# Fused local/global attention and top-1 expert layer on one core: the values' normalisation moved from TensorE's f32 transposes to VectorE's 32x32 block transposes

## The chip, the core and the metric

The kernel runs on one core of a Trainium2 chip. The metric is the device time of one execution in microseconds, the median of several. Unchanged, three runs gave a median of 1819.14 us (1817.94 to 1822.35).

## What is computed

The reference, cut to what matters here (x is 16 x 512 x 256, so 8192 tokens of 256 features):

```python
def mha(x, W_in, b_in, W_out, b_out, mask):      # 16 heads of 16
    q, k, v = heads(split(x @ W_in.T + b_in))
    scores = einsum('bhqd,bhkd->bhqk', q, k) / 4 + mask
    a = softmax(scores)
    o = einsum('bhqk,bhkd->bhqd', a, v)
    return o @ W_out.T + b_out
# local: windows of 128 tokens; global: windows of 256
fused = w[0] * local + w[1] * global             # w = softmax(fusion_w)
y = layernorm(fused) * gamma + beta
x = x + layernorm(y)
# then a top-1 mixture of 32 experts, 320 slots each, and x + layernorm(...)
```

All of it is f32 at the edges. The change touches only o: the quotient of the weighted values and the softmax denominators, in both attentions.

## The kernel before, in words

There are 32 windows of 256 tokens. The attention part is a software pipeline of 36 steps. In step s five windows are in work: `a` = s is projected to queries and keys, `b` = s-1 gets its row maxima and its value projection, `c` = s-2 gets scores, exponentials and the products with the values, `d` = s-3 gets the output projection and its two normalisations, `f` = s-4 gets router and slots. Steps 4 to 31 have all five. After the steps, 32 experts follow, which the change does not touch.

Each step is cut into 24 units k (`UNITS`). In unit k every engine walks through the same list of jobs, each job at the unit that the table `AT` (L271) or `GROUP_AT` (L276) gives it. Each engine's program is in order, so this hand-written table sets what waits behind what. A unit's frame is: TensorE makes a bank of scores of `c` (`scores`, L1091), then the jobs of that unit, then a bank of raw scores of `b` (`row_scores`, L1158); VectorE does its jobs and then the maximum of that bank (`maximum`, L883); ScalarE does the exponential of the first bank (`exps`, L674). The raw-score banks are two, so TensorE's `row_scores(k)` waits for VectorE's `maximum(k-2)`.

The values. For each window eight groups of four heads (four local, four global) are multiplied by TensorE into one PSUM bank, `PV`, [4 heads x 32 rows, 256 tokens]; of the 32 rows of a head 16 are the values and one is the softmax denominator (`values`, L1121). In the kernel before, ScalarE copies each group to `OT` (`values_out`, L676, line L681). TensorE transposes four groups at a time, 128 tokens, into bank `TR` (`norm_T`, L1202; four f32 transposes through L1184), VectorE takes the reciprocals of the denominators and multiplies (`normalise`, L899, lines L903 and L907), TensorE transposes back, four more (`out_T`, L1207), and ScalarE copies the result to `OnT` (`onT_out`, L726, line L730). The output projection `op` (L1275, units 9 and 10) reads `OnT`. Per window that is six sets of four transposes: n_g0, n_g1 and oT_g at units 3, 5 and 7, n_l0, n_l1 and oT_l at units 16, 18 and 20.

Other jobs that the prediction speaks of: `fbuf` (L985) reads the output projection, with statistics behind it (L821, L824); GpSimd (POOL) turns these into a standard deviation (`inv_std`, L533 to L540); ScalarE normalises (`f1` and `z`, L716); GpSimd scales and shifts (L583, L586). Queries and keys are split into three bf16 parts by ScalarE (L688), GpSimd (`remainder` L550, `low_part` L555) and VectorE (`mid_part`, L871). `split_maxima` (L885, lines L890 to L896) splits the row maxima; TensorE transposes them (L1199, `mT_g` and `mT_l`), ScalarE copies them (L724), and the SP queue carries them to the score operand (L427); the queue's other issues are mostly the spreading of the parts (L413, L422). `route_slot` (L932) has a product of two tiles in SBUF, L941. ScalarE's queue issues ten DMAs at the start (L645 to L651), on whose count VectorE waits at L846, before the output weights are scaled (L860) and the bias row is made (L866).

Of the kernel before, what the change touches and what calls it, by code (L numbers as in the profile page):

```python
# [8 lines left out]
def attention_moe_program(nc, T, x, pT_l, pT_g, winT_l, winT_g, woT_l, woT_g, bqk_l, bqk_g, bv_l, bv_g,  # L9
# [56 lines left out]
    with ExitStack() as ctx:  # L66
# [43 lines left out]
        OT = sb("OT", [P, 2, 4, WIN])  # L110
        rden = sb("rden", [P, 2, NH])
        On = sb("On", [P, 2, 2, D])
# [48 lines left out]
        with ExitStack() as experts:  # L161
# [54 lines left out]
        ot_ready = sem("ot_ready")  # L216
        nrm_full = [sem("nrm_full_l"), sem("nrm_full_g")]
        on_ready = [sem("on_ready_l"), sem("on_ready_g")]
        onT_full = [sem("onT_full_l"), sem("onT_full_g")]
# [424 lines left out]
        def _(act):  # L644
            act.dma_start(xw[:, 0, :, :], x_w[0]).then_inc(x_in[0], 16)  # L645
            act.dma_start(fus[:, :], fusion_w.partition_broadcast(P)).then_inc(wo_in, 16)
            for b, (o_, k_, v_, c_) in enumerate(((woT_l, bqk_l, bv_l, bo_l), (woT_g, bqk_g, bv_g, bo_g))):
                act.dma_start(bv[:, 2 * b:2 * b + 2], v_).then_inc(wo_in, 16)
                act.dma_start(bqk[:, b, :], k_).then_inc(wo_in, 16)
                act.dma_start(wo[:, 2 * b:2 * b + 2, :], o_.rearrange("(c p) n -> p c n", p=P)).then_inc(wo_in, 16)  # L650
                act.dma_start(bo[:, b, :], c_.partition_broadcast(P)).then_inc(wo_in, 16)  # L651
# [23 lines left out]

            def values_out(g, c):  # L676
                wait(act, pv_full, c, GROUPS, g)
                b = g // 4

                wait(act, nrm_full[b], back(c), 2, 1)  # L680
                act.activation(OT[:, b, g % 4, :], PV[:, 0:WIN], ACT.Copy).then_inc(ot_ready, 1)  # L681

# [43 lines left out]
            def onT_out(b, w):  # L726
                wait(act, onT_full[b], w)

                wait(act, o_full, back(w))
                act.activation(OnT[:, b, :, :].rearrange("p t n -> p (t n)"), TR[:, :], ACT.Copy).then_inc(onT_ready[b], 1)  # L730

            def step(s, par):
                a, b, c, d, f = stages(s)
                for k in range(UNITS):
# [11 lines left out]
                    if c and k in GROUP_AT:  # L746
                        values_out(GROUP_AT[k], c)
                    if d and k == LAST_GROUP_AT:
                        values_out(GROUPS - 1, d)
# [18 lines left out]
                    if d and k == AT["oT_g"]:  # L768
                        onT_out(1, d)
# [9 lines left out]
                    if c and k == AT["oT_l"]:  # L779
                        onT_out(0, c)  # L780
# [26 lines left out]
        def _(dve):  # L807
# [38 lines left out]
            dve.wait_ge(wo_in, 16 * 12)  # L846
# [52 lines left out]
            def normalise(b, q, w):  # L899

                wait(dve, nrm_full[b], w, 2, q)
                src = TR[:, :].rearrange("p (h m) -> p h m", m=32)
                dve.reciprocal(rden[:, b, :], src[:, :, HD])  # L903
# [56 lines left out]
            def step(s, par):  # L960
# [3 lines left out]
                for k in range(UNITS):  # L964
# [6 lines left out]
                    for q in range(2):  # L971
                        if d and k == AT[f"n_g{q}"]:
                            normalise(1, q, d)
                        if c and k == AT[f"n_l{q}"]:
                            normalise(0, q, c)
# [92 lines left out]
        def _(pe):  # L1068
# [113 lines left out]
            def four_transposes(src, sem_full):  # L1182
                for n in range(4):
                    last = pe.transpose(TR[:, n * P:(n + 1) * P], src(n), ident[:, :])  # L1184
                last.then_inc(sem_full, 1)

# [14 lines left out]

            def norm_T(b, q, w, s):  # L1202
                wait_read(pe, TR_USES, f"n_{'lg'[b]}{q}", s, 1)
                wait(pe, ot_ready, w, GROUPS, 3 + 4 * b)
                four_transposes(lambda n: OT[:, b, n, q * P:(q + 1) * P], nrm_full[b])

            def out_T(b, w, s):  # L1207

                wait_read(pe, TR_USES, f"oT_{'lg'[b]}", s, 1)
                wait(pe, on_ready[b], w, 2, 1)  # L1210
                four_transposes(lambda n: On[:, b, n % 2, n // 2 * P:(n // 2 + 1) * P], onT_full[b])
# [166 lines left out]
```

## Time and profile before

| | |
|---|---|
| median of the runs | 1819.14 us |
| the profiled execution, its own time | 1818.58 us |
| its span in the trace | 1816.8 us |
| TensorE (PE) busy | 90% |
| VectorE (DVE) busy | 68% |
| ScalarE (ACT) busy | 55% |
| GpSimd (POOL) busy | 49% |
| mean granted TensorE clock | 0.97 of 2.4 GHz |

How to read it: the trace lists each instruction's start and duration; a wait is the idle time of an engine before an instruction, with the one that released it. A span's busy share is an average over the start, the 28 full steps and the experts, so the stretches below are read one at a time. Times are us from the span's start; durations in the group lists are ns.

### The profile page before, as it was taken

To read this page: it belongs to the slowest core of one execution; us is meant where nothing else is said; L and a number is where in the kernel's file an instruction comes from. 1 tells how busy PE (TensorE), PEld (TensorE's weight loads), DVE (VectorE), ACT (ScalarE), POOL (GpSimd) and SP (SyncE) were. 2 spreads that over 40 slices of the span, in tenths; PEclk is the share of its full clock that TensorE was granted. 3 is DMA by queue.
4 is the path that set the end of the run, shared out by engine and by line. 5 is a ranking of instruction groups with operands and counts; after the bars stand their busy time and mean duration, and the time that the engine had idled before them with its cause. 6 is when DMAs were issued, how large, how long until landed. Compare 5 with 4: busy or idle time off the path is not lost.

```text
span 1816.8 us, 43072 instructions
## 1 busy us (share of the span) xinstructions
PE 1636.8 (90%) x14472; PEld 1184.8 (65%) x14472; DVE 1226.7 (68%) x3673; ACT 993.6 (55%) x2251; POOL 884.3 (49%) x1173
## 2 busy tenths in 40 slices
PE   5779999999999999999999999999999846999993
PEld 3457777777776676766676776777776634666662
DVE  2446777777777776777777777777777534777773
ACT  2356666666666666666666666666666531111210
POOL 3224545445445555545554444444444341666665
PEclk9789999999999999999999999999999967999997
DMA  6985555555555555555555555555555202444540
GB/s 138 222 181 98 95 96 97 96 95 96 97 94 96 96 96 94 95 94 94 93 92 91 91 93 94 94 92 94 92 84 97 67 13 74 146 138 140 153 126 10
DMA packets 254346, 183.59 MB, mean 101 GB/s; under 512 B 30116, under 2 KB 252775, under 8 KB 254142
## 3 DMA queue, kind: packets, MB, share of 16 engines
q1 hardware_dynamic: 245150, 176.22, 48.9%
q0 software_dynamic: 7168, 3.73, 1.2%
q8 instruction: 112, 1.84, 0.5%
q10 hardware_dynamic: 1824, 1.06, 0.2%
q14 instruction: 92, 0.75, 0.2%
HBM read 55.78 MB, written 38.04 MB: 52 GB/s over the span
## 4 chain that ended last, share of the span: by engine, by line
PE 59%; POOL 17%; issue 8%; DVE 6%; SPq 4%; ACT 3%; DVEq 2%; DMA 1%; POOLq 0%; ACTq 0%
PE bank L1147 11%; PE bank L1275 7%; PE bank L1184 5%; PE bank L1178 4%; PE bank L1129 4%; PE bank L1116 4%; PE bank L1137 3%; POOL out L632 3%; POOL zb L627 3%; PE bank L1175 3%; PE bank L1108 3%; PE bank L1104 3%; PE bank L1154 3%; SPq L422 2%; POOL ybuf L583 2%
## 5 line engine op out<-in xcount | busy, mean ns | idle before, releaser
L883 DVE TENSOR_REDUCE mx<-bank 128x2 f32<-128x512 f32 (+1 forms) x768 | 513.3, 685 | 134.1 <-PE bank L1175 87.2
L674 ACT ACTIVATE pt<-bank 128x512 f32<-128x512 f32 x768 | 448.2, 601 | 160.2 <-PE bank L1116 130.2
L550 POOL TENSOR_TENSOR rest<-x,parts 128x512 f32<-128x512 f32 x128 | 148.5, 1160 | 295.7 <-ACT x L688 295.7
L1147 PE MATMUL bank<-xnT,weff 128*128 128x256 f32 x1024 | 247.4, 385 | 2.4 <-ACT x L688 1.7
L1178 PE MATMUL bank<-stack 96*128 96x256 bf16 x1024 | 198.9, 276 | 20.6 <-DVE mx L883 19.6
L688 ACT ACTIVATE parts<-bank,bqk 128x256 bf16<-128x256 f32 x256 | 107.5, 471 | 173.4 <-PE bank L1147 160.4
L1147 PEld LDWEIGHTS bank<-xnT,weff 128*128 128x128 f32 x1024 | 185.9, 191 | 23.8 <-ACT x L688 2.1
L555 POOL TENSOR_TENSOR parts<-rest,parts 128x512 bf16<-128x512 f32 x128 | 148.4, 1160 | 107.7 <-DVE parts L871 107.7
L1116 PE MATMUL bank<-stack 100*128 100x128 bf16 x2048 | 198.9, 219 | 0.0
L1116 PEld LDWEIGHTS bank<-stack 100*128 100x128 bf16 x2048 | 158.9, 98 | 12.5
L1178 PEld LDWEIGHTS bank<-stack 96*128 96x128 bf16 x1024 | 79.5, 98 | 125.2 <-issue 57.4
L1113 PE MATMUL bank<-tri,identb 128*128 128x256 bf16 x512 | 141.3, 276 | 14.8 <-DMA stack<-mT 10.5
L533 POOL TENSOR_TENSOR nm<-mv,minus 128x2 f32<-128x2 f32 x96 | 18.8, 195 | 271.3 <-DVE mv L824 271.3
L1311 PE MATMUL bank<-eT,ew 128*128 128x320 f32 x512 | 148.3, 443 | 1.8 <-ACT eT L789 0.9
L871 DVE CAST parts<-rest 128x512 bf16<-128x512 f32 x128 | 54.0, 422 | 131.4 <-POOL rest L550 131.4
L1137 PE MATMUL bank<-pt,v_pad 128*32 128x256 f32 x2048 | 137.4, 386 | 0.5 <-ACT pt L674 0.5
L798 ACT ACTIVATE sg<-bank 128x320 f32<-128x320 f32 x64 | 28.0, 438 | 196.5 <-PE bank L1311 196.5
L1154 PE MATMUL bank<-weff,xnT 128*128 128x512 f32 x256 | 127.3, 620 | 5.4 <-ACT x L688 5.4
L1311 PEld LDWEIGHTS bank<-eT,ew 128*128 128x128 f32 x512 | 95.8, 192 | 49.9 <-issue 15.0
L1275 PE MATMUL bank<-wo,OnT 128*128 128x256 f32 x512 | 126.8, 392 | 0.6 <-ACT OnT L730 0.6
L681 ACT ACTIVATE OT<-bank 128x256 f32<-128x256 f32 x256 | 102.0, 398 | 43.7 <-PE bank L1137 42.6
L536 POOL TENSOR_TENSOR rstd<-ve,mhalf 128x2 f32<-128x2 f32 x160 | 112.7, 704 | 12.5
(149 smaller groups left out, 3144.3 us busy)
## 6 DMA issues: line engine op xcount, KB each, us to landing
stack<-parts SPq DMA_DIRECT2D x384, 128.0 KB, 6.7
stack<-parts SPq DMA_DIRECT2D x768, 64.0 KB, 2.6
slots_scratch<-zeros SPq DMA_DIRECT2D x5, 2080.0 KB, 11.9
erows<-slots_scratch SPq DMA_DIRECT2D x64, 130.0 KB
xr<-x SPq DMA_DIRECT2D x32, 256.0 KB, 7.2
out<-obuf SPq DMA_DIRECT2D x32, 256.0 KB, 2.1
ew<-w_gate SPq DMA_DIRECT2D x32, 256.0 KB, 3.2
ew<-w_up SPq DMA_DIRECT2D x32, 256.0 KB, 3.5
```

What stands on the lines that cost most here:

```text
L550: pool.tensor_tensor(rest[:, j % 2, :], x32[:, j % 2, :], parts[:, j, 0, :], ALU.subtract).then_inc(rest_ready, 1)
L555: pool.tensor_tensor(parts[:, j, 2, :], rest[:, j % 2, :], parts[:, j, 1, :], ALU.subtract).then_inc(lo_ready, 1)
L674: act.activation(pt[:, u % 8, :], S2[u % 2][:, :], ACT.Exp).then_inc(p_ready, 1)
L883: dve.reduce_max(dst, src, AX.X).then_inc(s1_read, 1)
L1113: pe.matmul(diagonal, identb[:, :], tri[:, :].unsqueeze(1).to_broadcast([P, 2, P]), start=True, stop=False)
L1116: last = pe.matmul(bank[:, (2 * kb + qb) * P:(2 * kb + qb + 1) * P], k_stack(par, 1, u - LU, kb * P, P, BROW), q_stack(par, 1, u - LU, qb ...
L1137: last = pe.matmul(PV[32 * h4:32 * h4 + 32, 0:WIN], v_pad[:, par, kb, 1, 4 * (g - 4) + h4, :], pt[:, (u0 + h4) % 8, kb * WIN:(kb + 1) * WI ...
L1147: last = pe.matmul(bank[:, t * WIN:(t + 1) * WIN], weff[:, b, c, qk * D + t * P:qk * D + (t + 1) * P], xnT[:, par, c, :], start=(c == 0), ...
L1154: last = pe.matmul(pj_bank(f"v{q}")[:, :], xnT[:, par, c, q * P:(q + 1) * P], weff[:, :, c, 2 * D:3 * D], start=(c == 0), stop=(c == 1))
L1178: last = pe.matmul(bank[:, n * WIN:(n + 1) * WIN], q_stack(par, 1, u - LU, n * P, P, NPART), k_stack(par, 1, u - LU, 0, WIN, NPART), start ...
L1275: last = pe.matmul(TR[:, q * D:(q + 1) * D], OnT[:, n // 2, n % 2, q * P:(q + 1) * P], wo[:, n, :], start=(n == 0), stop=(n == 3))
L1311: last = pe.matmul(banks[2 + 2 * m + n][:, 0:CAP], ew[:, e[1] % 3, n, c, m * P:(m + 1) * P], eT[:, e[1] % 2, c, :], start=(c == 0), stop=( ...
```

## The change

The values are normalised by VectorE alone. `unfold` reads `PV` right after `values` with a block transpose: each 32x32 block is transposed in place of its block, so that the 32 rows of a head become 32 adjacent numbers of a token. After every second group a reciprocal and a product follow, both now with all their tensors in SBUF. `fold` transposes a chunk of normalised values back, block by block. ScalarE's copies, TensorE's transposes and the table's entries for them go; `PV` is released by VectorE (`pv_read`). The order in which the values' rows end up differs from that of the output weights, so these and the value bias are loaded in pieces of 16 rows, in 32 DMAs in place of four. `fold_g1`, `fold_l0`, `fold_l1` and `fold_g0` get units 2, 11, 14 and 18; `mT_g` moves from unit 1 to 2, `top` from 3 to 4, `gate` from 5 to 6, `split_l` from 9 to 12, `mT_l` from 12 to 14.

```diff
-        TR_USES = [("mT_g", 2, mT_ready[1], 1, 0), ("n_g0", 3, on_ready[1], 2, 0), ("n_g1", 3, on_ready[1], 2, 1),
-                   ("oT_g", 3, onT_ready[1], 1, 0), ("op", 3, f_ready, 1, 0), ("mT_l", 1, mT_ready[0], 1, 0),
-                   ("n_l0", 2, on_ready[0], 2, 0), ("n_l1", 2, on_ready[0], 2, 1), ("oT_l", 2, onT_ready[0], 1, 0)]
+        TR_USES = [("mT_g", 2, mT_ready[1], 1, 0), ("op", 3, f_ready, 1, 0), ("mT_l", 1, mT_ready[0], 1, 0)]
...
-        AT = {"split_g": 0, "x2T": 0, "xnT": 0, "mT_g": 1, "lg": 2, "o_norm": 2, "p0": 3, "n_g0": 3, "top": 3, "p1": 5, "n_g1": 5,
-              "gate": 5, "oT_g": 7, "cs": 7, "op": 9, "split_l": 9, "p2": 10, "p3": 12, "mT_l": 12, "f1": 12, "v0": 15, "stats_y": 15,
-              "n_l0": 16, "z": 17, "n_l1": 18, "norm0": 18, "v1": 19, "stats_x1": 19, "oT_l": 20, "xn2": 21, "stats_xn2": 23}
+        AT = {"split_g": 0, "x2T": 0, "xnT": 0, "fold_g1": 2, "mT_g": 2, "lg": 2, "o_norm": 2, "p0": 3, "top": 4, "p1": 5,
+              "gate": 6, "cs": 7, "op": 9, "p2": 10, "fold_l0": 11, "split_l": 12, "p3": 12, "f1": 12, "fold_l1": 14, "mT_l": 14,
+              "v0": 15, "stats_y": 15, "z": 17, "norm0": 18, "fold_g0": 18, "v1": 19, "stats_x1": 19, "xn2": 21, "stats_xn2": 23}
...
-                act.dma_start(bv[:, 2 * b:2 * b + 2], v_).then_inc(wo_in, 16)
+                for h in range(4):
+                    for half in range(2):
+                        lo, at = 64 * half + HD * h, 32 * h + HD * half
+                        act.dma_start(bv[at:at + HD, 2 * b:2 * b + 2], v_[lo:lo + HD, :]).then_inc(wo_in, 16)
+                        act.dma_start(wo[at:at + HD, 2 * b:2 * b + 2, :], o_.rearrange("(c p) n -> p c n", p=P)[lo:lo + HD, :, :]
+                                      ).then_inc(wo_in, 16)
...
-            dve.wait_ge(wo_in, 16 * 12)
+            dve.wait_ge(wo_in, 16 * 40)
...
+            def unfold(g, w):
+
+                b, chunk, half = g // 4, g // 2 % 2, g % 2
+                if half == 0:
+                    dve.drain()
+                wait(dve, pv_full, w, GROUPS, g)
+                dve.transpose(otok[:, b, half, :], PV[:, 0:WIN]).then_inc(pv_read, 1)
+                if half == 1:
+                    src = otok[:, b, :, :].rearrange("p s (n m) -> p s n m", m=32)
+                    dve.drain()
+                    dve.reciprocal(rden[:, b, :, :], src[:, :, :, HD])
+                    dve.drain()
+                    dve.tensor_tensor(On[:, b, chunk, :].rearrange("p (n s d) -> p s n d", s=2, d=HD), src[:, :, :, 0:HD],
+                                      rden[:, b, :, :].unsqueeze(3).to_broadcast([P, 2, WIN // 32, HD]), ALU.mult)
+
+            def fold(b, chunk, w):
+
+                if chunk == 0:
+                    wait(dve, o_full, back(w))
+                dve.drain()
+                dve.transpose(OnT[:, b, chunk, :], On[:, b, chunk, :]).then_inc(onT_ready[b], 1)
...
-                wait(pe, ot_ready, c if g else back(c), GROUPS, (g - 1) % GROUPS)
+                wait(pe, pv_read, c if g else back(c), GROUPS, (g - 1) % GROUPS)
...
-                                wait(pe, onT_ready[0], d)
-                                wait(pe, onT_ready[1], d)
+                                wait(pe, onT_ready[0], d, 2, 1)
+                                wait(pe, onT_ready[1], d, 2, 1)
```

The functions `values_out`, `onT_out`, `normalise`, `four_transposes`, `norm_T` and `out_T` and their calls are removed; `unfold(g)` is called at the unit of `values(g)` (3, 5, 7, 9, 13, 17, 21, and 1 of the next step), `fold` at the units above.

## Rows read from the trace of the kernel before

**Rows 1.** Windows: us; PE, PEld, DVE, ACT, POOL busy; clock; DMA share; GB/s.

```profile
718.40:728.10 9.70, 9.70 (x92) 6.71 (x92) 5.29 (x12) 7.83 (x18) 7.16 (x9) 1.00 0.79 111
728.10:743.30 15.20, 13.02 (x138) 8.75 (x130) 14.20 (x42) 9.61 (x20) 6.66 (x14) 1.00 0.28 71
743.30:762.00 18.70, 18.70 (x197) 15.28 (x197) 11.97 (x41) 11.67 (x30) 7.91 (x7) 1.00 0.55 105
718.40:762.00 43.60, 41.42 (x419) 30.74 (x417) 31.46 (x94) 29.11 (x66) 21.73 (x30) 1.00 0.51 94
```

**Rows 2.** Instruction groups: busy us, mean ns, idle before, releasers.

```profile
L883 DVE TENSOR_REDUCE mx<-bank 128x2 f32<-128x512 f32 (+1 forms) x768 | 513.3, 685 | 134.1 <-PE bank L1175 87.2 <-PE bank L1178 42.4 <-issue 0.4
...
L681 ACT ACTIVATE OT<-bank 128x256 f32<-128x256 f32 x256 | 102.0, 398 | 43.7 <-PE bank L1137 42.6 <-PE bank L1129 0.9
...
L1184 PE MATMUL bank<-ident,OT 128*128 128x128 f32 x512 | 83.2, 285 | 30.5 <-DVE On L907 30.3
...
L907 DVE TENSOR_TENSOR On<-bank,rden 128x256 f32<-128x256 f32 x128 | 54.4, 425 | 9.9 <-issue 0.4
...
L903 DVE RECIPROCAL rden<-bank 128x16 f32<-128x16 f32 x128 | 31.4, 246 | 31.1 <-PE bank L1184 30.8 <-issue 0.2
```

**Rows 3.** Timeline of TensorE, same step: start, us, instruction, idle before it.

```profile
726.55 0.60 PE L1184 MATMUL bank<-ident,OT 128*128 128x128 f32 x4
726.99 0.38 PE L1178 MATMUL bank<-stack 96*128 96x256 bf16 x2
...
729.14 0.39 PE L1178 MATMUL bank<-stack 96*128 96x256 bf16 x2 [0.42 <-DVE mx L883]
...
730.76 0.65 PE L1184 MATMUL bank<-ident,OT 128*128 128x128 f32 x4 [0.89 <-DVE On L907]
...
741.96 0.27 PE L1199 MATMUL bank<-identb,mparts 128*48 128x128 bf16 x2 [0.83 <-issue]
```

**Rows 4.** Timeline of VectorE, from one output projection to the next.

```profile
718.37 0.69 DVE L985 TENSOR_TENSOR fbuf<-bank,bias_row 128x512 f32<-128x512 f32 x1 [1.45 <-PE bank L1275]
...
728.05 0.43 DVE L871 CAST parts<-rest 128x512 bf16<-128x512 f32 x1 [3.29 <-POOL rest L550]
...
754.78 0.88 DVE L941 TENSOR_TENSOR posh<-pos,hot 128x64 f32<-128x64 f32 x1
...
758.59 0.57 DVE L890 TENSOR_SCALAR mparts<-mx 128x32 bf16<-128x32 f32 x1
...
759.87 0.69 DVE L883 TENSOR_REDUCE mx<-bank 128x2 f32<-128x512 f32 x1
762.00 0.69 DVE L985 TENSOR_TENSOR fbuf<-bank,bias_row 128x512 f32<-128x512 f32 x1 [1.46 <-PE bank L1275]
```

**Rows 5.** Waits of VectorE in the third stretch: us, times, longest.

```profile
DVE mx L883 <- PE bank L1175: 2.5, 3, 1.2
DVE rden L903 <- PE bank L1184: 0.9, 1, 0.9
DVE pos L935 <- PE bank L1267: 0.8, 1, 0.8
```

**Rows 6.** Timeline of GpSimd, the same step.

```profile
750.71 1.27 POOL L565 TENSOR_TENSOR obuf<-obuf,xrow 128x512 f32<-128x512 f32 x1
...
754.43 1.16 POOL L550 TENSOR_TENSOR rest<-x,parts 128x512 f32<-128x512 f32 x1 [0.24 <-ACT x L688]
```

**Rows 7.** Timeline of the start: ScalarE's queue, VectorE and TensorE.

```profile
6.16 0.74 ACTq L651 DMA_DIRECT2D bo<-bo_g  x1
...
15.21 0.43 DVE L847 COPY bvb<-bv 128x512 f32<-128x512 f32 x1 [6.22 <-DMA bo<-bo_g]
...
24.39 0.63 PE L1230 MATMUL bank<-ident,xn 128*128 128x128 f32 x4 [0.82 <-DVEq L867]
```

**Rows 8.** The chain, early: landing of a maxima transfer.

```profile
100.45 4.30 DMA stack<-mT
```

**Rows 9.** Timeline of the SP queue, a full step.

```profile
746.12 0.75 SPq L427 DMA_DIRECT2D stack<-mT  x1
```

More of the change, by code:

```diff
@@ L109, in attention_moe_program @@
         mT = sb("mT", [48, 2, WIN], bf16)
-        OT = sb("OT", [P, 2, 4, WIN])
-        rden = sb("rden", [P, 2, NH])
-        On = sb("On", [P, 2, 2, D])
+        otok = sb("otok", [P, 2, 2, WIN])
+        rden = sb("rden", [P, 2, 2, WIN // 32])
+        On = sb("On", [P, 2, 2, WIN])
         OnT = sb("OnT", [P, 2, 2, WIN])
@@ L215, in attention_moe_program @@
         pv_full = sem("pv_full")
[L216 to L219, printed above, removed]
+        pv_read = sem("pv_read")
         onT_ready = [sem("onT_ready_l"), sem("onT_ready_g")]
@@ L674, in exps @@
                 act.activation(pt[:, u % 8, :], S2[u % 2][:, :], ACT.Exp).then_inc(p_ready, 1)
[L676 to L681, printed above, removed]
             def projected(j, a, dst):
@@ L724, in maxima_out @@
                 act.activation(mT[:, b, :], TR[0:48, 0:WIN // 2].bitcast(bf16), ACT.Copy).then_inc(mT_ready[b], 1)
[L726 to L730, printed above, removed]
             def step(s, par):
@@ L745, in step @@
                                        ).then_inc(xnT_ready, 1)
[L746 to L749, printed above, removed]
                     if c and k == AT["mT_g"]:
@@ L767, in step @@
                         last.then_inc(gsum_ready, 1)
-                    if d and k == AT["oT_g"]:
-                        onT_out(1, d)
                     if d and k == AT["f1"]:
@@ L778, in step @@
                             v_out(q, b, 1 - par)
-                    if c and k == AT["oT_l"]:
-                        onT_out(0, c)
             steps(act, step)
@@ L897, in split_maxima @@
                                   ).then_inc(mparts_ready[b], 1)
[L899 to L903, printed above, removed]
+            def unfold(g, w):
[14 more added lines that the diff above has]
+                    wait(dve, o_full, back(w))
                 dve.drain()
-                wait(dve, onT_full[b], back(w))
-                dve.tensor_tensor(On[:, b, q, :].rearrange("p (h d) -> p h d", d=HD), src[:, :, 0:HD],
-                                  rden[:, b, :].unsqueeze(2).to_broadcast([P, NH, HD]), ALU.mult).then_inc(on_ready[b], 1)
+                dve.transpose(OnT[:, b, chunk, :], On[:, b, chunk, :]).then_inc(onT_ready[b], 1)
             def route_top(d):
@@ L970, in step @@
                         route_top(f)
[L971 to L975, printed above, removed]
+                    if c and k in GROUP_AT:
+                        unfold(GROUP_AT[k], c)
+                    if d and k == LAST_GROUP_AT:
+                        unfold(GROUPS - 1, d)
+                    if d and k == AT["fold_g1"]:
+                        fold(1, 1, d)
+                    for chunk in range(2):
+                        if c and k == AT[f"fold_l{chunk}"]:
+                            fold(0, chunk, c)
+                    if c and k == AT["fold_g0"]:
+                        fold(1, 0, c)
                     for j in range(4):
@@ L1180, in row_scores @@
                 last.then_inc(s1_full, 1)
[L1182 to L1185, printed above, removed]
             def maxima_T(b, a, s):
@@ L1200, in maxima_T @@
                 last.then_inc(mT_full[b], 1)
[L1202 to L1211, printed above, removed]
             def step(s, par):
@@ L1245, in step @@
                         last.then_inc(lg_full, 1)
-                    for q in range(2):
-                        if d and k == AT[f"n_g{q}"]:
-                            norm_T(1, q, d, s)
-                        if c and k == AT[f"n_l{q}"]:
-                            norm_T(0, q, c, s)
                     if a and k == AT["p0"]:
@@ L1255, in step @@
                             project(j, a, s, par)
-                    if d and k == AT["oT_g"]:
-                        out_T(1, d, s)
                     if f and k == AT["cs"]:
@@ L1283, in step @@
                             project_v(q, b, s, 1 - par)
-                    if c and k == AT["oT_l"]:
-                        out_T(0, c, s)
                     if b:
```

1 line of the change is left out of this document (removed).

## The prediction

> **What bounds the kernel now.** I read one full step first, cut where the dependencies change hands [rows 1]: from the end of the output projection (718.4) to VectorE's last mid part (728.1), from there to the start of the next step's unit 1 (743.3), and on to the next output projection (762.0). A step takes 762.00 - 718.37 = 43.63 us [rows 4]. TensorE is busy in 41.42 us of it, VectorE in 31.46, ScalarE in 29.11, at a granted clock of 1.00 [rows 1]. That reads as a kernel bound by TensorE, and over the step it is; but not in each stretch.
>
> In the first stretch (9.7 us) VectorE stands still for 3.29 us before its last mid part, released by GpSimd [rows 4]. Behind that stands one fixed chain: output projection, `fbuf`, statistics, `inv_std`, `f1`, two gamma/beta products, `low_part(2)`, `remainder(3)`. In the second stretch (15.2 us) VectorE is busy for 14.20 us [rows 1], the rest being its drains, and all the step's waits of TensorE are there: 0.42 us for a maximum, 0.89 for the normalised values, 0.83 before the transposes of the maxima, which begin right when `split_maxima` ends, though the row calls it issue [rows 3]. So there VectorE sets the pace. In the third (18.7 us) TensorE is busy throughout [rows 1], and VectorE waits 2.5 + 0.9 + 0.8 us for it [rows 5] and 1.46 for the output [rows 4].
>
> **What goes from TensorE.** A set of four transposes moves the next instruction by 0.44 us (726.55 to 726.99) [rows 3]; the group's busy time, 83.2 us for 512, gives 0.65 a set as an upper bound, overlap counted in [rows 2]. I take 0.49, six sets a window, 2.9 us. One set lies in the first stretch, where the fixed chain governs, and gives nothing. Stretches two and three hold 33.9 us; without five sets (2.5) and the three waits (2.1), TensorE needs 29.3 there.
>
> The Trainium skill, "VectorE: DVE Perf Modes", The three transpose paths, gives TensorE 390 ns and VectorE 311 ns for a 128x128 bf16 transpose. By that TensorE would be freed of 24 x 0.39 = 9.4 us a window, which as an estimate would make the change a gain of several per cent; the row above decides against it, since pipelined transposes cost 0.12 us.
>
> **What goes from ScalarE.** Eight copies at 0.398 us [rows 2] and two larger ones. ScalarE is idle for a third of the step [rows 1]; its waits in the chain are for GpSimd. I count nothing.
>
> **What comes to VectorE.** Per window: eight block transposes PSUM to SBUF (128x256 f32), four inside SBUF, four reciprocals, four products, 16 drains; four reciprocals, products and drains go. The trace shows no block transpose. The nearest row is a 128x256 product that reads PSUM, 0.425 us; a lower bound is 0.35; an upper bound is the 128x512 pass at 0.685 us, which is what a second pass for 4-byte elements would cost [rows 2]. I take 0.44, by the row of the same shape. Neighbours without a drain overlap by 0.09 us and a drain costs about 0.08 between instructions (read off the gaps around L883 and L907). Then a first-half `unfold` is 0.50, a second-half one 0.44 + 0.19 + 0.43 + two drains = 1.08, a `fold` 0.47, and a removed `normalise` 0.246 + 0.425 [rows 2] + drain - overlap = 0.65.
>
> *Stretches two and three.* VectorE is occupied for 33.95 less its waits 4.2 [rows 5] and 1.46 [rows 4], 28.3 us. Added: four second-half unfolds (units 17, 1, 5, 9) 4.3, three first halves (21, 3, 7) 1.5, two folds (18, 2) 0.95; removed: four normalises 2.6 and `split_l`, 758.59 to 759.87, 1.3 [rows 4]. Sum 31.1. This is more than TensorE's 29.3, so VectorE becomes the bound of both stretches.
>
> *The shared reads.* A product that took its first input from PSUM now has both in SBUF. The same kind of instruction in the trace, `posh`, has 64 columns and took 0.88 us; it ended (755.66) when GpSimd's L550 (754.43 to 755.59) did [rows 4, 6]. So these products can be held by GpSimd. One, at unit 5, meets L550 and L565 (750.71, 1.27 us) [rows 6]; one, at unit 17, meets `inv_std` and `low_part`; at unit 1 GpSimd is idle. Bounds: 0, and two or three whole GpSimd instructions, 3. I take 0.9, since `split_l`'s first instruction loses its own hold (0.57 us for 32 columns [rows 4]). 31.1 + 0.9 = 32.0.
>
> *First stretch.* It gets `fold_l0`, `split_l`, a first-half unfold and `fold_l1`, 2.75 us, hidden in VectorE's 3.29 us plus smaller waits; that cover is nearly used up, and past it every us would be paid. `mT_l` two units later lets the SP queue start its next twelve spreads later, needed only eight or more units on. `mT_g` is issued at 746.12 [rows 9], behind twelve spreads, and an early one landed 4.30 us after [rows 8], so by 750.4; the first global scores stand at about 754.3. `mT_g` is behind the queue, not the queue behind it, and unit 2 instead of 1 costs nothing; 2 us of slack remain in the shorter step. What is queued behind VectorE's new wait for `PV` is the maximum of the same unit, thus TensorE two units on: `values` stands ahead of `row_scores` on TensorE, so the wait is short.
>
> *The step.* 9.7 + 32.0 + 0.4 for the mutual waits of two engines in near balance = 42.1, against 43.63: 1.5 us a step, 28 full steps, 42 us.
>
> **The start.** ScalarE's queue made ten issues by 6.90 us [rows 7], 0.6 each; 28 more take 17 us and end near 24. VectorE went on at 15.21, 9 us after the last issue, with the large weights in flight [rows 7]; later issues should land in 2 to 8. Then the weights' scaling, ScalarE's copies that wait behind the exponential, the bias product and row remain, 7 of the 9.2 us between VectorE's row and TensorE's first transposes (24.39) [rows 7]. So these move to 32 to 38. I take +9, bounds +6 and +14. Nothing hides it.
>
> **The last steps.** Three outputs come after the last full step, with the sets in a chain and no maxima; I take -6, bounds 0 and -12. The experts are untouched.
>
> Sum against the profiled execution's 1818.6 (0.5 under the median 1819.1): 1818.6 - 42 - 6 + 9 = 1779.6.
>
> **Rivals.** *Better.* The products meet no hold and the block transposes are at 0.40: 30.7 + 9.7 + 0.4 = 40.8, or with small holds 41; 2.6 x 28 = 73, so about 1745. TensorE's floor, 9.7 + 29.3 = 39.0, isn't reached. For it: GpSimd idles in half of the step [rows 1]. Chance 0.20; the forecast's own case 0.53.
>
> *No difference.* The holds cost 2.4 us in place of 0.9: 9.7 + 33.5 + 0.4 = 43.6, and start and end cancel; 1820. For it: `posh`, held by a whole GpSimd instruction in the full steps. Chance 0.09. The Trainium skill, "SBUF — State Buffer", Who interferes with whom, has the pair of ports that VectorE and GpSimd share as an exclusive lock held for a whole instruction; by that rule this is how it goes wherever GpSimd issues first, and the `posh` row agrees.
>
> *Slower.* The place is VectorE in stretches two and three, and the price of a 4-byte block transpose. At 0.69, the bound above, nine of them add 2.25: 9.7 + 34.3 + 0.4 = 44.4, 0.7 us more a step, +20, with the start and end +5: about 1843. It decides from 0.60 us each. Against it: nothing in the trace, only that VectorE's other f32 instructions take one pass. The Trainium skill, "Vector Engine (DVE) Microarchitecture Reference", 3.8 The reshape front-end, says that the transpose sustains one element per cycle per lane; no run here shows it. Chance 0.18.
>
> **How the numbers follow.** About 0.3% (5.5 us) is what a measurement of this kernel can tell from no change. Faster 0.73, within 0.3% 0.09, slower 0.18. The range goes from the better case, 1745, to just past no difference, 1822, and leaves out the slower case and what lies below the better one.
>
> **What would show it.** Right: a step of about 42.1 us, VectorE over 90% busy between its last mid part and the output projection, TensorE's waits for maxima grown there; block transposes at 0.40 to 0.46 us; L1230 at 32 to 38 us. Wrong: transposes at 0.6 or more; the products at 1 us or more; waits of TensorE for `mT`'s transfer at unit 8 (then the SP queue binds); VectorE no longer waiting for `remainder(3)` (then the first stretch has grown).

## The result: slower by 6.3%, and the profile after

The changed kernel takes 1934.1 us (median; 1933.0 to 1937.7) where the kernel before, measured beside it, takes 1820.05: a ratio of 1.063, 95% interval 1.061 to 1.065. Forecast were 1780 us and a range of 1745 to 1822. The profiled execution has a span of 1931.5 us against 1816.8, so 114.7 us more.

**Where they sit.** From one `fbuf` to the next a full step took 43.73 us in the mean of 28 (149.88 to 1374.29); now it takes 47.77 (156.88 to 1494.44), which is 28 x 4.04 = 113.1 us. The first `fbuf` comes 7.0 us later, and what follows the last full step (the end of attention and the experts) is 5.5 us shorter. 113.1 + 7.0 - 5.5 gives 114.6, the difference of the spans. So the steps are the question.

The windows of one full step of the changed kernel, cut at `fbuf`, at the start of VectorE's last mid part, at the last instruction of the other branch's `split_maxima`, and at the next `fbuf` (columns as in [rows 1]):

```profile
873.53:884.79 11.26, 8.52 (x64) 5.85 (x63) 9.90 (x19) 6.30 (x14) 7.15 (x9) 0.86 0.55 76
884.79:900.14 15.35, 13.61 (x142) 8.66 (x141) 13.45 (x41) 8.62 (x16) 6.31 (x13) 0.99 0.29 73
900.14:920.85 20.71, 19.06 (x194) 14.83 (x192) 16.96 (x49) 10.75 (x26) 8.31 (x9) 1.00 0.58 103
873.53:920.85 47.32, 41.19 (x395) 29.34 (x394) 40.32 (x107) 25.67 (x56) 21.78 (x30) 0.96 0.48 87
```

The kernel before at the same three marks (the second cut lies 1.6 us before that of [rows 1], at an instruction that both kernels have):

```profile
718.37:728.05 9.68, 9.68 (x91) 6.73 (x93) 5.27 (x11) 7.78 (x18) 7.16 (x9) 1.00 0.79 111
728.05:741.67 13.62, 11.73 (x125) 7.60 (x114) 12.76 (x40) 9.02 (x18) 6.18 (x13) 1.00 0.26 66
741.67:762.00 20.33, 20.04 (x210) 16.43 (x211) 13.45 (x44) 12.31 (x31) 8.39 (x9) 1.00 0.54 105
```

All three stretches grew: by 1.58, 1.73 and 0.38 us. TensorE is no longer busy throughout the first (8.52 of 11.26 us), and its granted clock there is 0.86, where it had been 1.00. Next comes what VectorE's instructions cost in the changed kernel (busy us, mean ns, idle before):

```profile
L883 DVE STREAM_TRANSPOSE otok<-bank 128x256 f32<-128x256 f32 x256 | 113.8, 444 | 21.1 <-PE bank L1124 5.5 <-PE bank L1132 4.7
L918 DVE TENSOR_SCALAR hot<-iota_e,idx_f 128x32 bf16<-128x32 f32 x64 | 62.2, 1014 | 2.8 <-issue 0.4
L889 DVE TENSOR_TENSOR On<-otok,rden 128x256 f32<-128x256 f32 x128 | 57.5, 449 | 10.2 <-issue 0.7
L897 DVE STREAM_TRANSPOSE OnT<-On 128x256 f32<-128x256 f32 x128 | 57.0, 445 | 11.9
L874 DVE TENSOR_TENSOR mparts<-mneg,mparts 128x32 bf16<-128x32 f32 x64 | 43.4, 678 | 5.1 <-issue 0.4
L872 DVE CAST mparts<-mneg 128x32 bf16<-128x32 f32 x64 | 42.3, 661 | 4.6
L868 DVE TENSOR_SCALAR mparts<-mx 128x32 bf16<-128x32 f32 x64 | 32.1, 501 | 6.5 <-issue 0.7
```

The new instructions cost what was forecast: both block transposes take 0.44 us, and the products 0.449 where those of [rows 2] took 0.425. What grew are 32-column instructions of old functions. The same ones before:

```profile
L890 DVE TENSOR_SCALAR mparts<-mx 128x32 bf16<-128x32 f32 x64 | 24.5, 383 | 6.1
L929 DVE TENSOR_SCALAR hot<-iota_e,idx_f 128x32 bf16<-128x32 f32 x64 | 12.4, 238 | 2.8 <-issue 0.4
L896 DVE TENSOR_TENSOR mparts<-mneg,mparts 128x32 bf16<-128x32 f32 x64 | 12.3, 192 | 4.8
L894 DVE CAST mparts<-mneg 128x32 bf16<-128x32 f32 x64 | 11.6, 181 | 4.7
```

`hot` went from 0.238 to 1.014 us, the last two of the split from 0.18 and 0.19 to 0.66 and 0.68 as a mean over both branches. Both belong to jobs that the change moved in the table: `top` from unit 3 to 4, `split_l` from 9 to 12. VectorE's timeline in the first stretch, and at `top`:

```profile
859.89 2.25 DVE L918 TENSOR_SCALAR hot<-iota_e,idx_f 128x32 bf16<-128x32 f32 x2
...
877.17 0.86 DVE L868 TENSOR_SCALAR mparts<-mx 128x32 bf16<-128x32 f32 x1
878.11 0.19 DVE L870 SCALAR_TENSOR_TENSOR mneg<-mx,mparts 128x32 f32<-128x32 f32 x1
878.37 1.24 DVE L872 CAST mparts<-mneg 128x32 bf16<-128x32 f32 x1
879.69 1.27 DVE L874 TENSOR_TENSOR mparts<-mneg,mparts 128x32 bf16<-128x32 f32 x1
...
882.03 0.39 DVE L849 CAST parts<-rest 128x512 bf16<-128x512 f32 x1
...
884.79 0.43 DVE L849 CAST parts<-rest 128x512 bf16<-128x512 f32 x1 [0.60 <-POOL rest L545]
```

GpSimd's timeline beside it:

```profile
859.72 1.15 POOL L545 TENSOR_TENSOR rest<-x,parts 128x512 f32<-128x512 f32 x1 [6.35 <-ACT x L680]
860.84 1.27 POOL L560 TENSOR_TENSOR obuf<-obuf,xrow 128x512 f32<-128x512 f32 x1
...
876.84 1.16 POOL L545 TENSOR_TENSOR rest<-x,parts 128x512 f32<-128x512 f32 x1
878.31 1.26 POOL L578 TENSOR_TENSOR ybuf<-fbuf,gamma_row 128x512 f32<-128x512 f32 x1 [0.32 <-ACT fbuf L708]
879.65 1.26 POOL L581 TENSOR_TENSOR ybuf<-ybuf,beta_row 128x512 f32<-128x512 f32 x1
882.50 1.15 POOL L550 TENSOR_TENSOR parts<-rest,parts 128x512 bf16<-128x512 f32 x1 [1.58 <-DVE parts L849]
```

I call it a hold when an instruction is lengthened in this way: each long VectorE instruction ends with one of GpSimd's, L868 at 878.03 with L545 (878.00), L872 at 879.61 with L578 (879.57), L874 at 880.96 with L581 (880.91), the pair of L918 at 862.14 with L560 (862.11). The Trainium skill, "SBUF — State Buffer", Who interferes with whom, has the shared ports as an exclusive lock held for a whole instruction; these rows agree. `split_maxima`, 1.3 us in [rows 4], takes 3.7 here. What stands behind it is then late: TensorE's transposes of the maxima, and VectorE's cast at 882.03, for which GpSimd stands still for 1.58 us. TensorE's timeline there:

```profile
881.06 0.27 PE L1189 MATMUL bank<-identb,mparts 128*48 128x128 bf16 x2 [2.46 <-issue]
...
882.64 3.16 PE L1149 MATMUL bank<-weff,xnT 128*128 128x512 f32 x4
```

TensorE stood for 2.46 us (the row calls it issue; the transposes of the maxima begin 0.10 us after L874 ends), and 0.6 us after it went on (at 881.7) its granted clock goes to the lower level, 1.2 GHz: the same four matmuls took 1.94 us at 841.34, and here they take 3.16. The clock falls like this in all 28 full steps of the changed kernel, and a second time in 7 of them. Over the span it is at that level for 237.5 us, against 114.6 before, when none of it lay between 108 and 1436 us, so in no full step. (The wait alone does not decide it, as a2 will show.)

### The profile page after: what moved, and what is told of

Read it like the earlier page. It is cut to its first block, busy times and chain, and to the rows that moved or that the text cites. A ratio compares the mean times of both kernels' runs of the same rounds, so it can differ in the third digit from the quotient of the medians.

```text
span 1931.5 us, 41510 instructions
## 1 busy us (share of the span) xinstructions
PE 1630.4 (84%) x13704; PEld 1140.8 (59%) x13704; DVE 1495.0 (77%) x4057; ACT 883.9 (46%) x1931; POOL 885.9 (46%) x1173
## 3 DMA queue, kind: packets, MB, share of 16 engines
q8 instruction: 105, 1.72, 0.4%
## 4 chain that ended last, share of the span: by engine, by line
PE 38%; DVE 30%; DVEq 13%; issue 7%; POOL 5%; SPq 4%; ACTq 1%; DMA 1%; ACT 1%; POOLq 0%
DVE mx L861 8%; PE bank L1142 6%; PE bank L1149 5%; PE bank L1281 4%; PE bank L1247 3%; DVE bst L799 3%; DVEq L800 3%; SPq L417 3%; PE bank L1173 3%; PE bank L1293 3%; DVEq L881 2%; DVEq L886 2%; DVE mparts L874 2%; DVE mparts L872 2%; PE bank L1132 2%
## 5 line engine op out<-in xcount | busy, mean ns | idle before, releaser
L1173 PE MATMUL bank<-stack 96*128 96x256 bf16 x1024 | 203.2, 281 | 86.0 <-DVE mx L861 85.5
L545 POOL TENSOR_TENSOR rest<-x,parts 128x512 f32<-128x512 f32 x128 | 148.0, 1156 | 276.6 <-ACT x L680 276.6
L1142 PE MATMUL bank<-xnT,weff 128*128 128x256 f32 x1024 | 254.3, 392 | 2.6 <-ACT x L680 1.7
L550 POOL TENSOR_TENSOR parts<-rest,parts 128x512 bf16<-128x512 f32 x128 | 153.5, 1199 | 206.4 <-DVE parts L849 206.4
L1111 PE MATMUL bank<-stack 100*128 100x128 bf16 x2048 | 204.2, 223 | 0.0
L1173 PEld LDWEIGHTS bank<-stack 96*128 96x128 bf16 x1024 | 75.5, 99 | 215.6 <-DVE mx L861 131.6
L1149 PE MATMUL bank<-weff,xnT 128*128 128x512 f32 x256 | 165.5, 782 | 6.9 <-ACT x L680 6.9
L883 DVE STREAM_TRANSPOSE otok<-bank 128x256 f32<-128x256 f32 x256 | 113.8, 444 | 21.1 <-PE bank L1124 5.5
L1170 PE MATMUL bank<-stack 96*128 96x128 bf16 x1024 | 101.9, 223 | 28.7 <-DVE mx L861 27.9
```

What stands on the lines that cost most here:

```text
L545: pool.tensor_tensor(rest[:, j % 2, :], x32[:, j % 2, :], parts[:, j, 0, :], ALU.subtract).then_inc(rest_ready, 1)
L550: pool.tensor_tensor(parts[:, j, 2, :], rest[:, j % 2, :], parts[:, j, 1, :], ALU.subtract).then_inc(lo_ready, 1)
L1111: last = pe.matmul(bank[:, (2 * kb + qb) * P:(2 * kb + qb + 1) * P], k_stack(par, 1, u - LU, kb * P, P, BROW), q_stack(par, 1, u - LU, qb ...
L1142: last = pe.matmul(bank[:, t * WIN:(t + 1) * WIN], weff[:, b, c, qk * D + t * P:qk * D + (t + 1) * P], xnT[:, par, c, :], start=(c == 0), ...
L1149: last = pe.matmul(pj_bank(f"v{q}")[:, :], xnT[:, par, c, q * P:(q + 1) * P], weff[:, :, c, 2 * D:3 * D], start=(c == 0), stop=(c == 1))
L1173: last = pe.matmul(bank[:, n * WIN:(n + 1) * WIN], q_stack(par, 1, u - LU, n * P, P, NPART), k_stack(par, 1, u - LU, 0, WIN, NPART), start ...
```

## The experiments

**Do the moved jobs carry the loss?** Three kernels put them back in the changed kernel and leave all else as it is.

```diff
 a1:  -"split_l": 12, "mT_l": 14      +"split_l": 9, "mT_l": 12
 a2:  -"top": 4, "gate": 6            +"top": 3, "gate": 5
 a3:  both
```

> The changed kernel with split_maxima of the local heads back at unit 9 and its transposes (mT_l) back at 12. Theory of the holds (small two-port or two-input VectorE instructions that fall beside GpSimd's gamma and beta products wait for whole GpSimd instructions, 3.7 us in place of 1.3, and TensorE waits 2.5 us for the result): step 47.4 to about 44.5 us, no wait before the maxima's transposes, granted clock near 1.00 in full steps, time about 1850 us. Rival, plain load (VectorE simply has 5.5 us more work in a step, wherever it stands): within 10 us of 1934.

> The changed kernel with the router's top at unit 3 and gate at 5, as before the change. Theory of the holds: hot (two comparisons of 128x32) goes from 2.25 to about 0.4 us, step 1 to 1.9 us shorter, 1880 to 1905 us. Rival, plain load: within 10 us of 1934.

> Both moves undone, so only the block transposes with their own jobs (and mT_g at unit 2) remain. Theory of the holds: step about 42.5 to 43.5 us, near the forecast's 42.1; 1790 to 1825 us. Rival, plain load of VectorE: above 1900 us.

Measured: a1 1868.6 us (ratio to the kernel before 1.0251, 1.0234 to 1.0269), a2 1896.1 (1.0412, 1.0395 to 1.0429), a3 1837.5 (1.0092, 1.0073 to 1.0110). The first stretch falls from 11.26 to 9.74 us when the split is back at 9; the third falls from 20.71 to 18.99 when `top` is back at 3. Together the moves were 97 of the 114 us. a1 and a3 came out above what was expected (1850, and 1825 at most), and a3 is still slower than the kernel before.

In a2 the split's hold is still there, and so, in each of its 28 steps, is the wait of 2.46 us of TensorE. In 13 of them the clock falls during it or within 2 us of its end, in 15 it does not fall at all. The first stretch of one of the 15:

```profile
849.43:860.70 11.27, 8.52 (x75) 5.92 (x74) 9.90 (x18) 6.93 (x16) 7.17 (x9) 1.00 0.67 87
```

So the first stretch is as long with the clock at 1.00 as with 0.86: what it gained in length is the hold's, and the clock's price comes later in the step.

**Do the moves cost that in the old kernel too?** The same edits the other way round, with no block transpose: b1 has the split moved, b2 `top`, b3 both.

```diff
 b1:  -"split_l": 9, "mT_l": 12       +"split_l": 12, "mT_l": 14
 b2:  -"top": 3, "gate": 5            +"top": 4, "gate": 6
```

> The kernel before with only split_maxima of the local heads at unit 12 and mT_l at 14; no block transposes. Theory of the holds: the four small instructions grow to about 3.6 us, TensorE waits for them at unit 14, step 43.6 to 45.5 or more, 1870 to 1900 us. Rival, plain load: VectorE has idle time there, so within 5 us of 1820.

> The kernel before with one thing changed: `top` goes from unit 3 to unit 4 and `gate` from 5 to 6, as the change has them. Undoing this pair took 38 us off the changed kernel (1934 to 1896). If the loss belongs to the unit itself (GpSimd is at the low part and the output's add there, and the two one-hot instructions of a pair stand behind it for about 1.0 us instead of 0.24), it must show in the old kernel too: those two at about 1.0 us, a step longer by 0.8 to 1.6 us, and 1842 to 1865 us. If it came only from the crowd of the changed VectorE order, the old kernel stays within 5 us of its own time.

> The kernel before with both moves of the table (`split_l` at 12 and `mT_l` at 14, `top` at 4 and `gate` at 6) and nothing else of the change. Theory: the moves are the loss, so this kernel without one block transpose loses most of the 97 us that undoing both gave back: by the sum of the single moves +17 (the split alone in the old kernel) and +20 to +40, so 1860 to 1890 us. If TensorE's clock falls in every step here as it does in the changed kernel, 1900 or more. Rival: the moves cost much only beside the 16 added VectorE instructions, and this kernel stays under 1850.

Measured: b1 1839.4 us (1.0098, 1.0078 to 1.0117), b2 1833.9 (1.0065, 1.0050 to 1.0080), b3 1848.7 (1.0150, 1.0135 to 1.0166). All three lie below what I had expected (1870, 1842 and 1860 at least). VectorE's groups in b3:

```profile
L929 DVE TENSOR_SCALAR hot<-iota_e,idx_f 128x32 bf16<-128x32 f32 x64 | 64.5, 1050 | 2.5
L896 DVE TENSOR_TENSOR mparts<-mneg,mparts 128x32 bf16<-128x32 f32 x64 | 43.3, 677 | 5.2 <-issue 0.4
L892 DVE SCALAR_TENSOR_TENSOR mneg<-mx,mparts 128x32 f32<-128x32 f32 x64 | 39.5, 618 | 5.1 <-issue 0.4
```

The holds are there too, but the moves cost 27 us in place of 97: the rival that I had put under 1850 us. So the holds belong to the places in the table. What they cost depends on the slack beside them, and `hot` shows it cleanly: its hold is as long in both kernels (1.050 and 1.014 us each), and in the third stretch it adds 0.51 us to the kernel before (20.34 to 20.85) and 1.72 to the changed one (18.99 to 20.71). In the first stretch the split's adds 0.37 (9.68 to 10.05) and 1.52 (9.74 to 11.26), but this pair is not clean: in the old kernel the moved split has two held instructions (L892 and L896), in the changed one three, and takes 2.9 us in place of 3.7. VectorE had 4.2 us of waits in the third stretch [rows 5] and 3.29 before its last mid part in the first [rows 4]; with the added block work 0.5 and 1.68 are left (r1 below).

**Which GpSimd instructions hold the split?** h1 is the changed kernel with the two gamma and beta products cut to 2 of 256 features a token; VectorE fills the rest with ones.

```diff
-  pool.tensor_tensor(ybuf[:, :, :], fbuf[:, :, :], gamma_row[:, :].unsqueeze(1).to_broadcast([P, 2, D]), ALU.mult
+  pool.tensor_tensor(ybuf[:, :, 0:2], fbuf[:, :, 0:2], gamma_row[:, 0:2].unsqueeze(1).to_broadcast([P, 2, 2]), ALU.mult
```

> The changed kernel, its maxima split left at unit 12, but GpSimd's gamma and beta products cut from 128x512 to 128x4 elements (they are left out of the result). Theory of the holds: the four instructions of split_maxima fall back to about 0.2 us each wherever they stood beside those products (mean 0.66 and 0.68 to 0.2 for the last two), and the fixed chain from fbuf to the last mid part loses 2.3 us besides. Rival (they are slow by themselves at this place, say by reading just-written tiles): the means stay at 0.66 and 0.68.

Measured: 1835.7 us (1.0080, 1.0058 to 1.0102). The cast is at 0.181 us again and the last subtraction at 0.195, while L868, held by L545, stays at 0.50 and `hot` at 1.01. The first stretch is 9.14 us and the second 14.42, at full clock (26 of 28 steps). In this 9.14 us GpSimd again stands still for VectorE's cast, for 1.57 us, so it is VectorE's own work with the split nearly unheld that sets it, and it is less than the 9.74 us of the whole chain: without these holds the split at unit 12 would have been hidden, as forecast (argued from this run; no run has the whole chain and no hold). The products that are left out also shorten GpSimd's chain, so this run names the holders, and its time is no clean measure of their price.

**What keeps a3 above the kernel before?** Three guesses: VectorE's added work (f1 cuts the four folds of a step to 32 of 256 columns), VectorE's load in general (m1 gives two normalisations to ScalarE), TensorE's clock (k1 adds twelve transposes of the identity a step, into a bank that is free then).

```diff
 f1: -  dve.transpose(OnT[:, b, chunk, :], On[:, b, chunk, :])
     +  dve.transpose(OnT[:, b, chunk, 0:32], On[:, b, chunk, 0:32])
 m1: -  ACT_NORMS = (1, 2, 4)
     +  ACT_NORMS = (0, 1, 2, 3, 4)
 k1: +  if c and b and k in (16, 18, 20):
     +      pe.wait_ge(mT_ready[0], nth(b, 1))
     +      for n in range(4):
     +          pe.transpose(TR[:, n * P:(n + 1) * P], ident[:, :], ident[:, :])
```

> a3_both_back with each fold's block transpose cut from 256 to 32 columns (the rest of the values is left out of the output projection, which stays at zero there). VectorE loses 4 x 0.23 us a step, two of them where I hold it to be the bound. Theory (VectorE's program is the bound between its last mid part and the output projection): the step shortens by 0.4 to 0.9 us, 1812 to 1828 us. Rival (TensorE or the chain of transfers is the bound): within 4 us of a3_both_back's 1837.

> a3_both_back with the normalisations of the next window's x and of x1 moved from VectorE to ScalarE (GpSimd makes the two further biases). VectorE loses 4 instructions, 1.3 us, between its last mid part and unit 0. Theory (VectorE is the bound there): step 1 us shorter, 1800 to 1815 us. Rival (ScalarE's exponentials are delayed behind the normalisations, or the step is bound elsewhere): 1830 us or more.

> a3_both_back with twelve transposes of the identity a step put back on TensorE at units 16, 18 and 20, where the kernel before had its own; their results are not read. Theory (TensorE's waits for maxima let its clock fall to 1.2 GHz for 3.4 us of nearly every step, and that costs 0.7 to 1 us): the half-clock stretches of the full steps go, and the time falls by 10 to 25 us although work is added. Rival (the clock costs nothing since VectorE is the bound): 0 to +15 us against a3_both_back.

Measured: f1 1836.7 us (1.0081, 1.0063 to 1.0099), nothing gained; m1 1846.8 (1.0142, 1.0110 to 1.0175), 9 us above a3. Both go against the theory that they tried, that VectorE's work alone sets the step. k1 1812.6 (0.9955, 0.9941 to 0.9970), 25 us less than a3 and less than the kernel before, by adding work to TensorE. One full step of a3, the longest of its 28 (44.96 us, where the mean is 44.28), cut at the marks used above:

```profile
866.98:876.72 9.74, 9.74 (x95) 6.45 (x93) 7.04 (x14) 7.78 (x17) 7.22 (x9) 1.00 0.93 125
876.72:891.13 14.41, 10.93 (x94) 7.49 (x90) 13.36 (x40) 6.51 (x12) 6.32 (x13) 0.88 0.24 60
891.13:911.94 20.81, 20.26 (x215) 15.53 (x215) 17.27 (x52) 11.25 (x27) 8.58 (x9) 1.00 0.60 105
```

and of k1:

```profile
854.86:864.59 9.73, 9.73 (x91) 6.73 (x93) 7.04 (x15) 7.55 (x17) 7.21 (x9) 1.00 0.82 120
864.59:879.01 14.42, 12.23 (x130) 8.03 (x123) 13.36 (x40) 7.28 (x14) 6.33 (x13) 1.00 0.26 65
879.01:898.38 19.37, 18.80 (x194) 14.67 (x192) 16.56 (x53) 10.65 (x26) 8.61 (x9) 1.00 0.62 109
```

With the transposes gone from units 16, 18 and 20, TensorE has gaps in the second stretch, and its clock there is 0.88. Here that stretch is no longer for it, since VectorE bounds it either way (14.41 and 14.42); TensorE comes out of it behind, and the third takes 20.81 us in place of 19.0 to 19.4. In k1 the clock holds in 27 of the 28 steps. Each kernel also has the other case in it: a3's two steps without a fall of the clock take 43.49 us in the mean, near k1's 43.32, and k1's one step with a fall takes 44.89. So it is the clock that the filler changes, not something else beside it. The same filler beside f1's and m1's edits, and in the changed kernel with its moves (there 16 more transposes just ahead of `mT_l`):

> k1_filler with the folds' block transposes cut to 32 columns (values left out of the output projection). Theory (VectorE bound, clock at 2.4 GHz): 0.5 to 0.9 us less a step, 1788 to 1800 us. Rival: within 3 us of k1_filler's 1812.6.

> k1_filler with the two normalisations on ScalarE (the edit of m1_norms_on_act). With the clock held up by the filler, theory (VectorE is the bound between its last mid part and the output projection, and m1 lost only because TensorE's clock kept falling): steps of 43.3 go to about 42.3 us, 1780 to 1795 us. Rival (VectorE's load there does not count, m1's loss was ScalarE's exponentials coming late): 1812 us or more.

> The changed kernel itself, its table untouched, with filler on TensorE: sixteen identity transposes before the transposes of the local maxima at unit 14, where TensorE waited 2.5 us, and four each at units 16, 18 and 20. Theory (part of the loss is TensorE's clock at 1.2 GHz for 3.4 us and more in every step): the half-clock stretches of full steps mostly go and the step falls from 47.4 to about 46.3 us, 1895 to 1915 us. Rival (VectorE's held instructions set the step alone): 1930 us or more.

Measured: n2 1802.8 us (0.9894, 0.9877 to 0.9911), 10 under k1: shorter folds are worth 0.3 us a step once the clock is held (0.23 of it in the second stretch), and nothing where it isn't. n1 1840.1 (1.0101, 1.0082 to 1.0120), 27 above k1: the norms on ScalarE stand ahead of exponentials that TensorE needs, and TensorE waits 0.62 and 0.90 us for these. TensorE, then ScalarE, in n1:

```profile
843.42 0.28 PE L1111 MATMUL bank<-tri,identb 128*128 128x256 bf16 x1 [0.62 <-ACT pt L673]
...
845.04 0.58 PE L1102 MATMUL bank<-tri,identb 128*128 128x512 bf16 x1 [0.90 <-ACT pt L673]
```

```profile
841.79 1.09 ACT L708 ACTIVATE xn<-xw,mr,rstd 128x256 f32<-128x256 f32 x2 [1.50 <-POOL mr L535]
...
843.33 1.09 ACT L708 ACTIVATE xn<-xrow,mr,rstd 128x256 f32<-128x256 f32 x2
```

The waits are the smaller part of the 27 us. Two steps of n1 that follow each other, one with a fall of the clock and one without:

```profile
1001.65:1046.75 45.10, 42.13 (x407) 30.54 (x406) 36.16 (x102) 27.45 (x60) 22.77 (x34) 0.96 0.52 91
1046.75:1090.29 43.54, 40.56 (x407) 29.32 (x406) 36.25 (x102) 27.20 (x60) 22.78 (x34) 1.00 0.52 95
```

12 of its 28 steps are of the first kind (45.17 us in the mean), 16 of the second (43.63); k1 has one and 27 (43.32). That makes about 17 us for the clock's falls and 9 for the rest, so the filler of k1 no longer holds the clock where ScalarE opens new gaps.

n3 1905.1 us (1.0450, 1.0434 to 1.0466), 29 under the changed kernel with 28 more transposes a step on TensorE. Its step of 46.43 us is 11.30 + 14.41 + 20.72, all at full clock, as in all its full steps: the holds stay, the clock's share is gone.

**The start, and the best version.** q1 permutes the output weights' rows and the value bias where the inputs are laid out, so that ScalarE issues four transfers in place of 32; it was tried on n1. r1 is k1 with it, r2 is r1 with `mT_g` at unit 1 as before.

```diff
 q1, r1:
-  act.dma_start(bv[at:at + HD, 2 * b:2 * b + 2], v_[lo:lo + HD, :]).then_inc(wo_in, 16)
...
+  act.dma_start(bv[:, 2 * b:2 * b + 2], v_).then_inc(wo_in, 16)
+  act.dma_start(wo[:, 2 * b:2 * b + 2, :], o_.rearrange("(c p) n -> p c n", p=P)).then_inc(wo_in, 16)
...
-  out[f"woT_{b}"] = np.ascontiguousarray(a[f"W{b}_out"].T)
+  out[f"woT_{b}"] = np.ascontiguousarray(a[f"W{b}_out"].T.reshape(2, 2, 4, 16, 256).transpose(0, 2, 1, 3, 4).reshape(256, 256))
 r2: -"mT_g": 2      +"mT_g": 1
```

> n1_filler_norms with the output weights' and value bias's rows put in the new order on the host, so that ScalarE's queue has ten issues again. Theory: TensorE's first transposes come at 24.4 instead of 32.1 us and everything after with them; 7 to 8 us less than n1. Rival (the start is hidden by later transfers): within 2 us of n1.

> The filler kernel (both moves undone, 12 identity transposes a step on TensorE, 1812.6 us) with the rows of the output weights and of the values' bias permuted where the inputs are laid out, so that the ScalarE queue issues four transfers for them instead of thirty-two. That took 5.0 us off another variant and brought its first new token 8.5 us earlier. Expected 1812.6 - 5 to 8 = 1805 to 1808 us, a ratio of 0.991 to 0.993 to the kernel before. If the start is hidden behind something later, 1812.

> The same as r1_best with the other branch's maxima transposes moved back from unit 2 to unit 1, where the kernel before has them. They stand ahead of the logits on TensorE, and their parts feed the first score rows. If the later place costs the stretch from the mid cast to the first unit anything, a step gets shorter by up to 0.3 us, 8 us in all: 1797 to 1807. If TensorE now waits at unit 1 for the split, which the first-unit order had avoided, it gets longer by 0.2 to 0.5 us a step: 1811 to 1820.

Measured: q1 1835.1 us (1.0076, 1.0062 to 1.0089), 5 under n1 where 7 to 8 were expected. r1 1806.8 (0.9917, 0.9904 to 0.9931): the fastest that computes everything, 0.8% under the kernel before. r2 1818.3 (0.9981, 0.9972 to 0.9990), 11.5 above r1; the third stretch is what grows (18.99 to 19.55): of the three moves the one of `mT_g` pays. A full step of r1 cut at the same marks, then the waits of VectorE and TensorE in its last two stretches:

```profile
630.04:639.78 9.74, 9.74 (x91) 6.73 (x93) 7.04 (x15) 7.56 (x17) 7.21 (x9) 1.00 0.78 119
639.78:654.19 14.41, 12.23 (x130) 8.03 (x123) 13.36 (x40) 7.27 (x14) 6.33 (x13) 1.00 0.26 65
654.19:673.18 18.99, 18.63 (x194) 14.74 (x192) 16.45 (x52) 10.65 (x26) 8.61 (x9) 1.00 0.61 107
```

```profile
DVE mx L857 <- PE bank L1166: 0.5, 1, 0.5
PE bank L1169 <- DVE mx L857: 2.2, 4, 1.0
```

The products are held now and then after all, 9 of the 112 in r1's full steps. One of them, and the GpSimd instruction that ran when it began (it ends at 446.84, the product 0.28 us later):

```profile
445.57 1.27 POOL L560 TENSOR_TENSOR obuf<-obuf,xrow 128x512 f32<-128x512 f32 x1
445.86 1.25 DVE L885 TENSOR_TENSOR On<-otok,rden 128x256 f32<-128x256 f32 x1
```

This is the product at unit 5 beside the output's add, the meeting that the prediction named. Its step takes 43.49 us in place of 43.14.

## Why the prediction was wrong, by its own steps

The mean step of 47.77 us now comes apart: 43.43 for the change with its clock nearly always held and the two moved jobs in their old places (r1, 151.16 to 1367.29, by 28), + 1.53 for the split's hold in the first stretch (11.27 in a2, 9.74 in a3), + 1.72 for `hot`'s in the third (20.71 in a1, 18.99 in a3), and 1.09 left for the clock, where n3 took 29 us by 28, or 1.04, off the changed kernel.

- **The failed step is the costing of what was moved.** In "First stretch" I took `fold_l0`, `split_l`, an unfold and `fold_l1` at 2.75 us, "hidden in VectorE's 3.29 us". `split_l` went in at its old 1.3 us and costs 3.7 in its new place. `top` had no term at all: the change moved it, and I only read that it moved. "The shared reads" has the mechanism and its rows, but asks the question of the new products alone, which met almost none of it (0.449 us). [rows 6] even had the output's add, `obuf` (750.71), the second of the two GpSimd instructions that now hold `hot`. What the runs showed in its place: 1.53 us a step for the split's hold and 1.72 for `hot`'s, 91 us in all (n3 less k1, with filler in both, is 92.5).
- **No term for the clock.** "TensorE needs 29.3" in stretches two and three, against VectorE's 32.0, leaves TensorE idle for longer than before; that its granted clock can fall then wasn't priced. In the second stretch it was busy in 11.73 of 13.62 us before and is in 10.93 of 14.41 in a3. The 114.6 us at the low level before, all of it outside the full steps, could have raised the question. Shown by k1, 25 us, and n3, 29 us.
- **One credit that isn't there.** The sum took 1.3 us off the third stretch for `split_l`. The stretch is 18.99 us with the split in it (a3's shortest, k1) and without it (a2's shortest): in [rows 4] it stood ahead of VectorE's own 1.46 us wait for the output. So VectorE is the bound of the second stretch and not, as forecast, of the third: there TensorE is busy in 18.63 of r1's 18.99 us, VectorE in 16.45, and n2's fold there, 0.23 us shorter, takes 0.07 off it. Without this credit the sum for stretches two and three is 33.7; r1 has 33.4. That they are so near is partly luck: the 0.9 of holds in the sum was 0.34 in r1's step above (`posh` at 1.22 us in place of 0.88, no held product). The change without the two moves' holds and without a lower clock is then a step of 43.14 against 43.63, a gain of 0.5 and not 1.5.
- **Right:** a block transpose at 0.44 us (0.444 and 0.445 measured), which throws out the rival "Slower" and its 0.69; that the kernel came out slower, as this rival has it, is chance: its reason was another, and so was its size (1843). VectorE as the bound of the second stretch. The first stretch at 9.7 with the split left out (9.74), and its cover for an unheld split (h1). The last steps -6 (-5.5). `mT_g` at unit 2 costs nothing; it gains (r2). The start, +9 forecast and +7.0 at the first `fbuf`; TensorE's first transposes come at 32.12 us, where 32 to 38 was forecast. Two rows of the changed kernel:

```profile
20.09 0.45 ACTq L650 DMA_DIRECT2D bo<-bo_g  x1
...
32.12 0.63 PE L1209 MATMUL bank<-ident,xn 128*128 128x128 f32 x4 [0.82 <-DVEq L845]
```

- "No difference" was the hold itself, at 2.4 us and on the products. It is nearer in kind than any other case, but it still put the hold in the wrong place and stopped at 1820.

What stays open: when the clock falls. The steps differ in length with its falls (a2's 15 without one take 44.81 us in the mean, the 3 with one 46.33, the 10 with two or more 47.38), but behind the same wait of 2.46 us it falls in one step of a2 and not in the next, by no pattern that I could name. Open too is whether some other unit for `split_l` and `top` would beat the old ones; none was tried.

## What to carry to other kernels

A job that is moved in the table has to be costed against what the other engines do in its new place: if it shares ports with GpSimd, lay the two timelines on each other at the new unit, for the smallest instructions too. A hold costs what slack does not cover (`hot`'s 0.51 us a step before and 1.72 in the changed kernel), so work that fills an engine's waits also raises the price of every hold and late start behind it. And where work leaves TensorE, ask for its clock: before counting its idle time as a gain, look at which stretch would have gaps, and try cheap filler there.

## What was not expected of the hardware

- Added work made the kernel faster: twelve f32 transposes of the identity a step, 0.61 us for four (the trace lists them as matmuls), took 25 us off. The Trainium skill, "TensorE: Matmul & The Clock Gate", Part 4: PE-mode transpose, says that transposes don't engage the full clock as other work does. These runs differ: with such transposes as the only work that was added, the granted clock stays at 1.00 in the step of k1 shown above, where a3 has 0.88, so for them the measurement decides. No run has transposes alone on TensorE.
- A 128x32 cast or subtraction takes 1.24 or 1.27 us where GpSimd has just begun a 128x512 instruction of 1.26 us, nearly seven times its own 0.18 or 0.19.
- An f32 block transpose of 128x256 costs the same out of PSUM (0.444 us) and out of SBUF (0.445), and none was held: the longest took 451 and 448 ns. One of 128x32 took 0.211 us (n2), so the 224 further columns cost 1.04 ns each. 61 of the changed kernel's 128 folds began while a 128x512 instruction of GpSimd ran, and none of these is longer either (minimum, median and maximum in ns; first and last start):

```profile
L897 DVE STREAM_TRANSPOSE OnT<-On x128: 445/445/448, 119.4 to 1587.5; 128x256 f32<-128x256 f32 x128
```
